# Probabilities turned in blocks of every fourth column, and brought back in one transfer

## The reference, cut to what matters

```python
def _L1_gnn_ref(h, adj, Wq, bq, Wk, bk, Wv, bv, Wo, bo):
    q = split_heads(h @ Wq.T + bq)
    k = split_heads(h @ Wk.T + bk)
    v = split_heads(h @ Wv.T + bv)
    scores = jnp.einsum('bhqd,bhkd->bhqk', q, k) * scale
    scores = jnp.where(mask, -jnp.inf, scores)
    attn = jax.nn.softmax(scores, axis=-1)
    out = jnp.einsum('bhqk,bhkd->bhqd', attn, v)
    out = out.transpose(0, 2, 1, 3).reshape(b, n, D_MODEL)
    return out @ Wo.T + bo

x = _layernorm(x + _L0_gnn_ref(x, adj, L0_gnn_W, L0_gnn_a), axis=-1)
x = _layernorm(x + _L1_gnn_ref(x, adj, ...), axis=-1)
```

## Time and profile before

| | |
|---|---|
| median of 3 runs | 3178.0 us (3174.58 to 3180.0) |
| span of the profiled execution | 3177.6 us |
| TensorE busy | 2986.1 us, 94% |
| VectorE busy | 2630.0 us, 83% |
| ScalarE busy | 2481.0 us, 78% |
| GpSimd busy | 2079.3 us, 65% |
| mean granted clock of TensorE | 0.983 of full speed |
| DMA engines busy | 75% |

### The profile page before, as it was taken

How to read it: one execution, slowest core, us unless ns; L and a number is a source line. 1 busy time by engine, 2 the same in 40 slices (tenths; PEclk the granted TensorE clock), 3 DMA queues, 4 the chain that set the end, 5 groups by cost and what they waited for, 6 DMA issues and landing times.

```text
span 3177.6 us, 60582 instructions
## 1 busy us (share of the span) xinstructions
PE 2986.1 (94%) x19084; PEld 2513.6 (79%) x19084; DVE 2630.0 (83%) x6553; ACT 2481.0 (78%) x5543; POOL 2079.3 (65%) x1927
## 2 busy tenths in 40 slices
PE   5899999999999999999999999999999999999995
PEld 4788888887888887788887887887888877888874
DVE  4788888888888888888888888888888888888874
ACT  3778788777788877888778887777888877888764
POOL 1566676666766666766667766666766666766664
PEclk7999999999999999999999999999999999999997
DMA  3677887777877777887777787777777778877765
GB/s 123 193 220 220 222 230 221 212 218 208 232 231 222 216 218 205 232 230 219 215 215 218 225 235 207 214 212 221 224 228 223 212 216 223 228 221 223 206 198 148
DMA packets 290047, 681.92 MB, mean 215 GB/s; under 512 B 40512, under 2 KB 74048, under 8 KB 256960
## 3 DMA queue, kind: packets, MB, share of 16 engines
q1 hardware_dynamic: 289728, 678.05, 75.0%
HBM read 375.40 MB, written 302.51 MB: 213 GB/s over the span
## 4 chain that ended last, share of the span: by engine, by line
PE 42%; DMA 25%; POOL 9%; DVE 8%; ACT 8%; SPq 3%; issue 3%; ACTq 0%; DVEq 0%; POOLq 0%
PE R_bank L724 27%; DMA turned_lo_prob<-scratch 12%; DMA scratch<-blocked 9%; PE O_bank L813 8%; POOL turned_lo_prob L1163 7%; PE S_bank L794 5%; DVE blocked L1105 3%; DMA r_wide<-r_scratch 3%; ACT turned_hi_prob L841 3%; SPq L628 3%; PE L_bank L715 2%; ACT prob L927 2%; POOL o_half L1158 1%; DVE qk_pair L1002 1%; ACT o_half L946 1%
## 5 line engine op out<-in xcount | busy, mean ns | idle before, releaser
L1163 POOL TENSOR_TENSOR turned_lo_prob<-turned_lo_prob,turned_hi_prob 128x512 fp32r<-128x512 f32 x1024 | 1297.1, 1297 | 564.0 <-ACT turned_hi_prob L841 563.2
L927 ACT ACTIVATE prob<-prob,small_cols 128x512 f32<-128x512 f32 x1024 | 729.8, 714 | 152.2 <-DVE small_cols L1085 143.9
L841 ACT ACTIVATE turned_hi_prob<-turned_lo_prob 128x512 fp32r<-128x512 f32 x1024 | 596.6, 622 | 228.1 <-DMA turned_lo_prob<-scratch 218.4
L1105 DVE STREAM_TRANSPOSE blocked<-prob 128x512 f32<-128x512 f32 x1024 | 692.4, 695 | 76.3 <-ACT prob L927 40.3
L1085 DVE CUSTOM_DVE_ANT_0 prob<-S_bank,mask 128x512 f32<-128x512 f32 x1024 | 677.2, 680 | 24.1 <-PE S_bank L794 20.1
L813 PE MATMUL O_bank<-turned_hi_prob,v_st 128*128 128x256 f32 x2048 | 528.2, 294 | 86.9 <-POOL turned_lo_prob L1163 83.6
L813 PE MATMUL O_bank<-turned_lo_prob,v_st 128*128 128x256 f32 x2048 | 513.6, 287 | 0.0
L813 PEld LDWEIGHTS O_bank<-turned_hi_prob,v_st 128*128 128x128 f32 x2048 | 398.3, 195 | 136.8 <-POOL turned_lo_prob L1163 125.3
L794 PE MATMUL S_bank<-qk_pair 64*128 64x512 f32 x3072 | 445.6, 416 | 16.3 <-DVE small_cols L1085 9.3
L724 PE MATMUL R_bank<-wv,x1T 128*128 128x256 f32 x3072 | 401.3, 286 | 1.6 <-DVE v_st L984 1.5
L813 PEld LDWEIGHTS O_bank<-turned_lo_prob,v_st 128*128 128x128 f32 x2048 | 399.6, 195 | 3.4
(11 more groups left out here) (90 smaller groups left out, 4390.0 us busy)
## 6 DMA issues: line engine op xcount, KB each, us to landing
scratch<-blocked SPq DMA_DIRECT2D x256, 1024.0 KB, 4.6
turned_lo_prob<-scratch SPq DMA_DIRECT2D x1024, 256.0 KB, 5.5
tokens<-xT SPq DMA_DIRECT2D x128, 256.0 KB, 4.8
tokens<-x SPq DMA_DIRECT2D x128, 256.0 KB, 3.8
r_wide<-r_scratch SPq DMA_DIRECT2D x512, 64.0 KB, 3.4
out<-tokens SPq DMA_DIRECT2D x128, 256.0 KB, 4.0
r_scratch<-r_cols SPq DMA_DIRECT2D x256, 2.0 KB
tokens<-adj SPq DMA_DIRECT2D x1, 1024.0 KB, 6.5
```

The lines of the kernel that those rows point to most:

```text
L841: act.activation(dst, src, ACT.Copy).then_inc(done, 1)
L927: act.activation(prob_tile(R, s), prob_tile(R, s), ACT.Exp, bias=negmax[:, slot:slot + 1], scale=-1.0, accum_out=psum_row[:, ph % 2, j:j + ...
L1105: dve.transpose(blocked[:, ph % 2, :, :, 2 * (s % 2) + s % 4 // 2, :].rearrange("p d c i -> p c d i"), prob_tile(R, s).rearrange("p (c d i ...
L1163: pool.tensor_tensor(turned_lo_prob[:, ph % 2, a, :, :], turned_lo_prob[:, ph % 2, a, :, :].bitcast(F32), turned_hi_prob[:, a, :, :].bitca ...
```

## The change

The transpose reads `prob` in another order. Before, one of its 32x32 blocks took 32 neighbouring keys (key = 128c + 32d + i, for block d and row i of the turned block). After, a block takes every fourth key of 128 (key = 128c + 4i + d). Row i of block d in partition group a so holds key 4i + d. `scratch` gets the same bytes at the same places in memory as far as its shape goes (partition, then d, then 512 values), but it can now be read as 128 rows of 512 values for each of the 4 query blocks a, in the order of the keys. One transfer over 128 partitions then takes the place of the four over 32. Its semaphore takes the place of four.

```diff
-        scratch = nc.dram_tensor("scratch", [4, P, 4 * N], F32, kind="Internal").ap()
+        scratch = nc.dram_tensor("scratch", [4, 4, P, N], F32, kind="Internal").ap()
...
-        p_moved = [[sem(f"p_moved{i}{a}") for a in range(4)] for i in range(2)]
+        p_moved = [sem(f"p_moved{i}") for i in range(2)]
...
             def store_probs(R, ph):
                 if due(R.n(8, ph - 3)):
-                    for d in range(4):
-                        sp.wait_ge(*moved(R, ph - 4, d))
+                    sp.wait_ge(*moved(R, ph - 4))
                 sp.wait_ge(p_turned, R.n(32, 4 * ph + 4))
-                sp.dma_start(scratch[ph % 4, :, :],
+                sp.dma_start(scratch[ph % 4, :, :, :].rearrange("a (j d) x -> (a j) (d x)", d=4),
                              blocked[:, ph % 2, :, :, :, :].rearrange("p d c j i -> p (d c j i)")).then_inc(p_stored[ph % 2], 16)
 
             def load_probs(R, ph):
                 sp.wait_ge(*stored(R, ph))
-                by_key_block = scratch[ph % 4, :, :].rearrange("(a j) (d x) -> d j a x", a=4, d=4)
-                for d in range(4):
-                    sp.dma_start(turned_lo_prob[BLK * d:BLK * (d + 1), ph % 2, :, :, :].rearrange("p a c x -> p a (c x)").bitcast(F32),
-                                 by_key_block[d]).then_inc(moved(R, ph, d)[0], 16)
+                sp.dma_start(turned_lo_prob[:, ph % 2, :, :, :].rearrange("p a c x -> p a (c x)").bitcast(F32),
+                             scratch[ph % 4, :, :, :].rearrange("a p x -> p a x")).then_inc(moved(R, ph)[0], 16)
...
                 if a == 0:
-                    for d in range(4):
-                        act.wait_ge(*moved(R, ph, d))
+                    act.wait_ge(*moved(R, ph))
...
                 dve.transpose(blocked[:, ph % 2, :, :, 2 * (s % 2) + s % 4 // 2, :].rearrange("p d c i -> p c d i"),
-                              prob_tile(R, s).rearrange("p (c d i) -> p c d i", c=T, i=BLK)).then_inc(p_turned, 1)
+                              prob_tile(R, s).rearrange("p (c i d) -> p c d i", c=T, i=BLK)).then_inc(p_turned, 1)
```

More of the change, by code:

```diff
@@ L564, in score_bank, with moved @@
             return S_bank[s % 4]
-        def moved(R, ph, d):
-            return p_moved[ph % 2][d], 16 * ((8 * R.k + ph) // 2 + 1)
+        def moved(R, ph):
+            return p_moved[ph % 2], 16 * ((8 * R.k + ph) // 2 + 1)
         def sums_loaded(R, ph):
```

## The result

The changed kernel takes 3238.94 us (median of 4 runs, 3235.92 to 3239.1), the kernel before beside it 3176.29. The ratio is 1.019, with a 95% interval of 1.0173 to 1.0207. It is slower, by 63 us where 172 were forecast (3350 − 3178), a little over a third.

A forecast was written before the change was run, and what follows sets the result against it. TensorE bounds the middle before; after the change VectorE would. 3177.6 + 175 (middle) − 3 (start and end: +5 for transposes, −8 for shorter trips) = 3350 us; range for all cases 3115 to 3430, its own 3290 to 3440.

The forecast's parts named there:

- the sum: Middle stretch: VectorE's work grows from 2428.15 to 2914 us, plus 111 us idle gives 3025; in all 3350 us.
- partial price: VectorE's transpose costs 0.25 us more, TensorE stays the bound; 3190 to 3290 us, say 3230; chance 0.13.
- the price of a transpose: VectorE's transpose, reading values 16 bytes apart, pays a full extra step for each: 0.51 us more, 1.21 us.
- the shorter trip: Probabilities' way through DRAM: one wide load saves 2 us a trip; 8 us at start and end beside a full VectorE.
- bound from GpSimd's row of 1297 ns: Upper limit for the transpose's extra time, from GpSimd's slowest pass over the same 128x512: 0.60 us over 695 ns.
- two loops: VectorE waits in the middle expected to stay: `x1T` 77.4 us and `blocked` for `exp` 33.3 us.
- first rival: VectorE's transpose stays at 695 ns and the shorter loads save 45 us: 3133 us, 3100 to 3168; chance 0.32.
- reciprocal's 7 ns: VectorE's reciprocal writing 128 bytes apart: 7 ns for each further value, read as a small sign that wide steps cost.
- The step costs nothing: Transpose reads 16 bytes apart at no extra time, loads save 45 us: 3133 us, 3100 to 3168; chance 0.32.
- Nothing moves: Transpose step free, the 1 MB load bounded by the DMA engines and landing at 6.8 us: 3178 us; chance 0.06.
- A part of the price: VectorE's transpose takes 0.25 us more, 93.5% busy in the middle under TensorE: 3190 to 3290 us; chance 0.13.
- likeliest case: VectorE becomes the bound with a transpose of about 1.2 us: 3350 us, most of it 3290 to 3440; chance 0.49.

The follow-up runs named there:

- step-only kernel: The kernel before with the transpose reading every fourth column, its four loads kept; keys in another order: 3318.35 us, ratio 1.0449.
- two pads: Plain transposes and one wide load, plus an unread VectorE maximum before each transpose, over 240 or 320 columns: 3187.18 and 3231.62 us.
- two-load kernel: Against the kernel before, the transpose reads every second column and two loads over 64 partitions replace four; computes the reference's attention: 3149.44 us, ratio 0.9907.

## Why the prediction was right and where it was wrong

**Right in sign, and in a part of the mechanism.** The two values 16 bytes apart do cost VectorE time, and VectorE became the engine that others wait for: it is 48% of the chain. But the sum's reason, work of 2914 us that doesn't fit into the 2850 of the old middle, so that VectorE and not TensorE is the bound, did not come. VectorE works 2739 us in the middle, less than TensorE's 2758. The case that came lies between two of mine. By the first row that I named to decide it, 1097 ns lies between the 950 of the partial price and the 1200 of the forecast. By who is fuller it is the partial price, by the chain the forecast.

The waits that I named for TensorE, `small_cols` and `x1T` in place of GpSimd's low parts, did not come either. The low parts stay first with 47.7 us, `small_cols` is one wait of 1.3 us, `x1T` holds 31.2 us where the loop through `L_bank` held 33.0. What is new are `qk_pair` (27.9 and 19.8 us) and `v_st`:

```profile
PE L_bank L712 <- DVE x1T L980: 21.7, 30, 0.7
PE S_bank L791 <- DVE qk_pair L998: 19.8, 30, 1.0
PE R_bank L721 <- DVE v_st L980: 17.5, 31, 2.6
PE L_bank L721 <- DVE x1T L980: 9.5, 29, 0.4
```

The granted clock, for which I had left room, did not fall: 0.986 over the span against 0.983.

**The steps that failed: the price of a transpose, and the shorter trip put at next to nothing once VectorE is full.** The experiments split the miss of 111 us (3350 against 3239):

- The step. I gave it 175 us in the middle and 5 at the ends, 180 in all. Alone it costs 141: 39 too much.
- The trip. Beside a VectorE that is the bound I gave it nothing in the middle and 8 us at the ends. With the step in both kernels it is worth 79 (3318 to 3239): 71 too little.

So the larger part of the miss is the overlap that I assumed: that VectorE, once full, hides the trip. The step-only kernel refutes it.

The price in the first term was wrong too. I put 512 x 1.00 ns = 0.511 us on a transpose, one full extra step for each value. It is 0.402 us (1097 − 695), 0.79 ns for each value. On 951 transposes the difference is 951 x (0.511 − 0.402) = 104 us. Put into the same sum, 0.402 gives 2428 + 382 + 111 = 2921 us for the middle and 3178 + 71 − 3 = 3246 us in all, 7 us over the measured 3239. That agreement is luck. The same sum without the 8 us of the loads gives 3254 us for the step-only kernel, which took 3318. The sum makes the step 64 us too cheap and the trip 71 us too cheap, and the two cancel. The bound from GpSimd's row of 1297 ns was further off still.

**What else was wrong inside the sum.**

- VectorE's work. The transposes' durations grew by 1024 x 0.402 = 412 us, but VectorE's busy time, in which time covered by two instructions counts once, grew by 336. The durations of all its instructions, added up from the traces, grew by 384 (2990.6 to 3374.8): others got shorter, one group of 64 (L994 before, L990 after) from 639 to 304 ns each, for a reason that is open. The other 48 us are time that two instructions cover. In the middle VectorE works 2739 us, not 2428 + 382 = 2810.
- The idle time that VectorE keeps. I kept 111 us in two loops; it is 171 (2910 − 2739). The two loops hold 82 of it (56.9 and 25.1). `h` and `qk_pair` shrank as I said, to 19.5 and 0.8, and `o_half`, which I hadn't counted, holds 24.9. The time of this kernel is not the work of its fullest engine plus a fixed rest: TensorE at 94.8% and VectorE at 94.1% hold up each other. The two pads show the cost rising gradually, 0.31 and then 0.6 us for each us of work on VectorE.
- The trip with VectorE free. It is worth 74 us (3177 to 3103) where I had capped it at 60, with the idle time for one wait of TensorE in the middle and 8 us at the ends. That wait fell by 37 us over the span (83.6 to 46.3), TensorE's idle time by 62 and its busy time by 14. And the trip is 2.6 us shorter, not 2, since the store lands sooner too.

Some readings of the prediction need a correction. Its end of 3460 us belongs to a price of 0.51 us and a VectorE 93% busy; with the 0.60 that it names beside it the same sum gives some 3550. The lower end of 3115 leaves out a fifth of the first rival's 3100 to 3168, not a third. The adjacency matrix is a fifth transfer of the new load's shape in the prologue, 6.5 us. And the reciprocal's 7 ns for each value written 128 bytes apart was no guide: 512 values written so by the reduce cost 0.83 ns each.

**The load.** Its duration was right (5.6 us against 5.3, a saving of 2.03 against 2). The reason is the 128 partitions and not the one transfer: four loads over 128 partitions give the same time, 3103.6 us. The Trainium skill's sentence in SBUF — State Buffer, "Door 1: The DMA port swizzle", that transfers over 32 or 64 partitions reach half of the ports, agrees with this, and with the packets of the 64-partition loads, which last as long as those over 32. No run here shows ports as such.

**The rivals.** "The step costs nothing" falls, by the row of 1097 ns; its time would have been 3103 us. "Nothing moves" falls. "A part of the price" named 0.25 us and 3190 to 3290 us; the price was 0.40 us, and the time lay in its range. It was nearer to the truth than my likeliest case in its time (3230 against 3350), and in the price a little less so. The Trainium skill's rule on 16-byte lines (same page and section) agrees in kind: steps of 4 and 8 bytes 695 ns, 16 bytes 1097. Its rule gives no ground for the further rise to 1186 ns at 32 bytes. The Trainium skill goes on in that note that how far one can stride for free depends on the type, "4 fp32"; read as a step of four values, that does not agree with the 1097 ns. In both the measurement decides.

**What stays open.** Why the extra is 0.79 ns for each value at 16 bytes and 0.96 at 32, why a VectorE that is nearly full doesn't hide the trip, and what brings the two-load kernel its 29 us. No kernel here computes the reference's attention and gets the whole 74 us of the load: it would need V's rows or K's columns reordered instead of the probabilities, which wasn't tried.

## What to carry to other kernels

Price an access pattern by the bytes between two values, where they are read and where they are written, before counting what the new layout saves on the other side: on VectorE 8 bytes were free here, 16 cost 58% of an instruction that runs 1024 times. Other engines were not measured. Bring transfers to 128 partitions first and worry about their number later: four loads cost no more than one. And when one engine gets fuller while another is the bound, expect neither zero nor the whole: here the added work cost 0.3 us for each us at first and 0.6 near the end, and a gain elsewhere kept its worth (74 us and 79).

## What the runs showed of the hardware

- STREAM_TRANSPOSE of 128x512 fp32 by the step of its reads: 695 ns at 4 bytes, 695 at 8, 1097 at 16, 1186 at 32. At 32 bytes the blocks come in another order too. A masked reduce writing at 128 bytes: 1106 ns against 680.
- The same bytes in the same number of packets took 75.0% of the DMA engines' time with loads over 32 partitions and 63.1% with loads over 128. A packet of 2 KB took 135 ns in the mean with loads over 32 partitions, 133 over 64 and 99 over 128. The untouched store beside them landed in 4.1 us instead of 4.6; with the narrow loads and a wide step it landed in 4.3.
- Issuing four loads instead of one cost SP 1.37 us for each half pair and the kernel nothing (3103.6 against 3103.2 us). Issuing the store in four took 2.87 us of SP's queue at the median.
